# The last attention group with its probability-by-value products in pairs, each pair behind the scores of two steps

## What is computed

```python
xn = layernorm(x)
s = attention(xn)            # 32 heads of 16, ALiBi bias, causal softmax, output projection
g = silu(ffn(xn))            # three octonion-structured ternary linear layers
return x + s * g
```

```python
scores = q @ k.T * scale + alibi        # causal mask
attn = softmax(scores)
out[:, h] = attn @ v
s = out @ w_out.T + b_out
```

## Time and profile before

| | |
|---|---|
| median of 3 runs | 831.38 us (829.61 to 833.06) |
| the profiled execution | 832.83 us, of which the span of its instructions is 831.0 us |
| PE busy | 795.5 us (96%) |
| DVE busy | 607.0 us (73%) |
| ACT busy | 473.9 us (57%) |
| POOL busy | 172.2 us (21%) |
| granted PE clock, mean | 0.996 |

### The profile page before, as it was taken

The page is one execution under the profiler, slowest core; times in us unless marked ns, Lnnn a source line. Parts: engine busy times, 40 slices in busy tenths (PEclk is TensorE's granted clock), DMA queues, the critical chain, the costliest instruction groups (busy, mean ns, idle before and its releaser), DMA issues.

```text
span 831.0 us, 16157 instructions
## 1 busy us (share of the span) xinstructions
PE 795.5 (96%) x5927; PEld 351.1 (42%) x5927; DVE 607.0 (73%) x1743; ACT 473.9 (57%) x633; POOL 172.2 (21%) x214
## 2 busy tenths in 40 slices
PE   5989999999999999999899999999999999999988
PEld 3545444444444444444334343344443334443333
DVE  6736887643232463563799999999999999996546
ACT  6425384332232222232488898888888888887540
POOL 3223222233434424434200000000000003530000
PEclk9999999999999999999899999999999999999999
DMA  7474422268202101101121122222225233652736
GB/s 265 134 212 166 140 102 77 104 146 292 89 1 88 64 1 39 64 0 46 57 80 54 58 65 79 80 79 68 61 66 167 75 112 101 194 151 100 224 130 220
DMA packets 71104, 88.40 MB, mean 106 GB/s; under 512 B 26898, under 2 KB 37150, under 8 KB 70512
## 3 DMA queue, kind: packets, MB, share of 16 engines
q1 hardware_dynamic: 70992, 87.36, 32.9%
q0 software_dynamic: 32, 0.01, 0.0%
HBM read 51.15 MB, written 35.93 MB: 105 GB/s over the span
## 4 chain that ended last, share of the span: by engine, by line
PE 70%; DVE 17%; DMA 5%; issue 4%; ACT 2%; POOL 1%; SPq 0%; DVEq 0%; ACTq 0%
PE psum L1560 12%; PE psum L1583 9%; PE psum L1517 9%; PE psum L1584 9%; DVE mx L1235 9%; PE psum L1594 5%; PE psum L1595 5%; PE psum L1535 4%; DVE mshown L1231 3%; PE psum L1409 2%; PE psum L1411 2%; PE psum L1410 2%; PE psum L1544 1%; PE psum L1619 1%; DMA o_scr<-osum 1%
## 5 line engine op out<-in xcount | busy, mean ns | idle before, releaser
L949 ACT ACTIVATE probs<-psum,exp_scale 128x1024 f32<-128x1024 f32 (+1 forms) x320 | 310.6, 1029 | 69.7 <-PE psum L1544 49.9
L1231 DVE CUSTOM_DVE_ANT_0 mshown<-psum,ahead 128x384 bf16<-128x384 f32 (+3 forms) x512 | 220.3, 487 | 2.7 <-PE psum L1517 0.4
L1517 PE MATMUL psum<-QKs 51*128 51x512 f16 (+3 forms) x768 | 185.6, 332 | 15.0 <-DVE mx L1235 6.5
L1560 PE MATMUL psum<-probs,Vs 128*32 128x512 f32 (+3 forms) x1536 | 162.1, 510 | 0.2 <-ACT probs L949 0.2
L1235 DVE TENSOR_REDUCE mx<-psum 128x1 f32<-128x512 f32 x256 | 157.5, 681 | 2.7 <-PE psum L1517 1.7
L1535 PE MATMUL psum<-QKs 53*128 53x512 f16 (+3 forms) x768 | 138.2, 329 | 1.6 <-ACT probs L949 1.4
L1583 PE MATMUL psum<-X,room 128*128 128x512 f16 (+1 forms) x352 | 133.6, 379 | 0.0
L1584 PE MATMUL psum<-X,room 128*128 128x512 f16 (+1 forms) x352 | 133.4, 379 | 0.0
L1517 PEld LDWEIGHTS psum<-QKs 51*128 51x128 f16 x768 | 52.0, 93 | 151.4 <-DVE mx L1231 78.1
L981 ACT ACTIVATE room<-psum,gate_half 128x512 f32<-128x512 f32 (+1 forms) x44 | 30.2, 687 | 101.6 <-PE psum L1584 101.5
L1258 DVE SCALAR_TENSOR_TENSOR room<-room,psum 128x512 f32<-128x512 f32 (+1 forms) x44 | 30.2, 687 | 63.2 <-ACT room L981 63.2
(11 more groups left out here) (166 smaller groups left out, 964.6 us busy)
## 6 DMA issues: line engine op xcount, KB each, us to landing
o_scr<-osum SPq DMA_DIRECT2D x32, 256.0 KB, 3.1
QKs<-q_scr SPq DMA_DIRECT2D x96, 64.0 KB
QKs<-k_scr SPq DMA_DIRECT2D x96, 64.0 KB
q_scr<-qk_stage SPq DMA_DIRECT2D x16, 256.0 KB, 2.7
k_scr<-qk_stage SPq DMA_DIRECT2D x16, 256.0 KB, 2.2
v_scr<-v_stage SPq DMA_DIRECT2D x16, 256.0 KB, 2.1
Vs<-v_scr SPq DMA_DIRECT2D x16, 256.0 KB
probs<-in_L_attn_x SPq DMA_DIRECT2D x4, 1024.0 KB, 11.1
```

Of the source, the lines that this page charges most:

```text
L949: nc.scalar.activation(probs[n % PSLOTS][:, 2 * pair:2 * pair + 2, 0:COLS[n]], s_bank[pair][:, :, 0:COLS[n]], ACT.Exp, scale=exp_scale[:, ...
L1231: last = nc.vector.tensor_tensor_reduce(out=mshown[tiles_read(at) % 2][:, cols], in0=m_bank[bank][:, cols], in1=ahead[:, CH - keys:], scal ...
L1517: last = nc.tensor.matmul(tile[:, hh, :], Qs[s][rows, pair + hh, qb * P:(qb + 1) * P], Ks[s][rows, pair + hh, k0:k0 + keys], start=(hh == ...
L1560: last = nc.tensor.matmul(pv_bank[32 * h:32 * h + 32, CH - cols:CH], Vs[s][:, kb, h::QH], probs[n % PSLOTS][:, h, at:at + cols], start=(kb ...
```

## The change

In the last group the order no longer comes from `GROUP` but from a string of its own, `CLOSING`. In it an S stands for both pairs of a step, a P for the product run of one step. The work is the same, and so is the number of pieces of projection ahead of the scores; only the order differs. Products 8 and 9 of group 14 stand together, then 1 and 2, 3 and 4, 5 and 6, and 7, 8, 9 of group 15.

```diff
+CLOSING = "PSPPSSPSSPPSSPPSSPPS"
+
+
+def closing_order():
+
+    t = QUADS - 1
+    products = [(t - 1, n) for n in range(NST - LAG, NST)] + [(t, n) for n in range(NST - LAG)]
+    out, n = [], 0
+    for kind in CLOSING:
+        if kind == "P":
+            out.append(("products", *products.pop(0)))
+        else:
+            out += [("scores", t, n, pair) for pair in range(2)]
+            n += 1
+    return out
+
+
 def work_order():
 
...
             pieces.sort(key=lambda w: w != ("scores", 0, 0, 0))
+        if t == QUADS - 1:
+            pieces = closing_order()
         for w in pieces:
             if t == QUADS - 1 and w[0] == "scores":
                 for piece in range(behind, min(behind + 1 + (behind == 0), PIECES)):
```

## The result

| | kernel before | changed kernel |
|---|---|---|
| median | 830.92 us (20 runs) | 834.62 us (20 runs) |
| ratio of the times, 95% interval | | 1.0037 (1.0023 to 1.0052) |
| profiled execution | 832.83 us, span 831.0 us | 836.05 us, span 834.2 us |

The account below looks back on a forecast made before the run. PE, 96% busy, was taken to bound the kernel, its end hanging on the later of transfers and PE. PE's 1.51 us delay fitted into 1.72 spare: 831.38 plus 0 plus 0.2 gave 831.6 us, range 829.6 to 834.2.

Parts of the forecast that it names:

- likeliest case: End of the kernel: all delays absorbed, time 830 to 832.6 us; chance 0.72.
- Part 1: Two products in a row on PE: the second saves 0.18 us; a pair of 512 columns takes 1.88.
- Part 2: Group's head: moving product 8 of group 14 costs nothing; first exponential 0.43 us earlier, only ACT waits for PE there.
- Part 3: Products 1 and 2 of group 15: PE 0.18 us earlier, copy of chunk 0 and its store 1.55 us later.
- Part 4: Store of chunk 0 of group 15: queued behind token loads, so its later issue adds 0; bounds 0 and +1.55 us.
- Part 5: Steps 5 to 9 of group 15, ACT setting the pace: two waits of ACT make product 9 come 1.51 us later.
- PE's spare time: Projection row 8: PE's 1.72 us wait for transfers absorbs the 1.51 us delay; 0.2 us added for shorter waits.
- The clock rival: PE in 788 to 792: thin work halves the clock, 1.8 to 2.8 us net, time 833.2 to 834.2; chance 0.09.
- the store rival: Store of chunk 0: lands later, moving the closing transfers by up to 1.55 us, time 832.9; chance 0.12.

Follow-up runs that it names:

- e3: Changed kernel's order with throwaway matmuls added in PE's waits of steps 6 and 8 (2.4 us of work); ratio 1.0021 to the kernel before.
- e1: Kernel before with only the head changed: product 8 of group 14 moved from behind product 7 to before product 9; ratio 1.0003.
- e4: Kernel before with the last two token loads (2 MB) issued behind the reciprocals of chunk 0 of group 15; ratio 0.9990.
- e2: Kernel before with only steps 5 to 9 changed: products 3 and 4, and 5 and 6, paired behind four scores calls; ratio 1.0043.
- e5: Kernel before with products 3 to 6 of group 15 each one place later, none paired; ratio 1.0014.
- e7: Changed kernel's order with throwaway matmuls only in the first pair's waits (step 6), none in step 8; ratio 1.0052 to the kernel before.
- e8: Changed kernel's order with the last three of twelve projection pieces held back for PE's waits in steps 6 and 8; ratio 1.0003 to the kernel before.
- e6: Kernel before with the last two token loads (2 MB) issued behind the reciprocals of chunk 1 of group 15; ratio 1.0015.

## Why the prediction was wrong in its likeliest case and right in a rival

**Part 1, right at full clock.** Products 1 and 2 ran in one stretch of 1.46 us, as the changed kernel's timeline shows (784.65 to 786.11), and a pair of 512 takes 1.88 at full clock (e3):

```profile
784.65 1.53 PE L1579 MATMUL psum<-probs,Vs 128*32 128x256 f32 x24
786.11 0.39 PE L1638 MATMUL psum<-OW,room 128*128 128x512 f16 x1
```

**Part 2, not refuted by the times, wrong in its reason.** I wrote that nobody waits for the first scores but ACT. PE itself does, for the load of the row maxima, which I had not looked up. It was covered in five of six profiles and cost 1.03 us in the sixth. e1 shows no cost in the median.

**Part 3, right.** From the end of product 9 of group 14 to the first scores of step 5 it is 17.81 us (787.51 - 769.70) against 17.98 before. The store was issued 1.55 us later, counted from the same place (786.87 - 769.70 = 17.17 against 785.03 - 769.41 = 15.62); 1.55 was forecast.

**Part 4, right in its cause, open to about 1 us in its size.** e4 shows that the loads held the store. Whether the landing stayed where it was can't be read from one pair of profiles. Counted from the last scores of group 14, the load behind the store came at 34.26 us in the changed kernel, against 34.86 before. But in e1, e2 and e5, which issue the store at 23.4 as before, it came at 32.7 to 32.9, and in e3 and e7, which issue it at 24.96, at 33.6 and 34.0. In the changed kernel it did not matter, since PE came last.

**Part 5, right in form, short of the clock: the step that failed.** The waits of ACT cost 1.60 (e3), forecast 1.51. What failed is that this part costs PE's work behind a wait at the durations of rows at full clock: it has 1.88 us for each pair, and they took 3.29 and 3.57 at a clock of 0.50. The sum that I made was 1.51; the measured one is:
- head wait 1.09 (in this execution only);
- waits of ACT 1.60;
- clock under products 3 and 4: 42.36 - 39.66 = 2.70, less the 1.09 = 1.61;
- clock under products 5 and 6: 1.62.

These sum to 5.92. They close by construction: the first and third terms together are the distance between the changed kernel and e7. The first agrees with the timelines, where group 15's first scores come 5.26 us after the last ones of group 14 in the changed kernel and 4.16 in e1 and e7. PE's spare 1.72 takes up its part, which leaves 4.2 us, where the two spans differ by 4.0 from group 14 on.

**The sum's other step, PE's spare time, was too long.** I let 1.72 us take up the 1.51 and added 0.2 for executions with a shorter wait. The wait was 0.91 in e1, and e3, with the clock at full, is 0.3 to 3.2 us slower than the kernel before. So more than 0.2 shows even without the clock; how much is not settled.

**The rivals.** The clock rival named the place, the cause and the price, 1.8 to 2.8 us net for one long fall. In the profile there were two short ones, of some 3.4 us each, at 1.6 each. I gave it 0.09 and leaned on a row that did not compare: in the wait of 1.72 us the clock stayed, but PE was busy on both sides of it (2.00 of 2 us in 804 to 806, 1.89 in 808 to 810). The row that did compare was the one of 400 to 404, with 2.28 of 4 us busy and the clock at half behind it; my own schedule gave 2.4 of 4 us for 788 to 792, nearly that, and 2.39 were measured. It should have been a likely case. The Trainium skill, TensorE: Matmul & The Clock Gate, What's actually happening, says that the clock is throttled by default and released by activity; the runs agree: e3 adds 2.4 us of useless work and gets 1.6 us per pair back.
In the profile the store rival did not decide the end, and the pairs did save their 0.18 us at full clock.

**How well this gives the time.** With the clock's price from the traces and without the head's wait, the sum is 1.60 + 3.23 - 1.72 = 3.1 us, or 834.0 to 834.5 from the two medians of before. That is near the measured 834.62, but some of it is luck. With e1's 0.91 for the spare time it is 3.9. And the average execution lost less clock than the profiled one: the stretches of 790 to 802 add up to 3.4 us of full clock lost, 0.0041 of the span, where the mean clock of the changed kernel's 20 executions is 0.0022 below that of the kernel before in e1's measurement. That is worth 1.8 us by an estimate (0.0022 of 831), and the sum is 1.7 to 2.5. The measured 1.9 to 4.3 us do not decide between these.

## What to carry to other kernels

When an order groups work for its own sake, look at what stands ahead of the group: a stretch in which PE only issues short matmuls between waits for another engine is paid twice, once as wait and once at half clock in the dense work behind it. Price such a stretch by a place in the same trace that looks like it, short work between waits over several us, not by a single gap between busy stretches. If the order is wanted, keep independent work (here projection pieces) for the waits instead of spending it all earlier: e8 has the same pairs and no loss that its interval (0.15% to each side) can show. And where a forecast lets spare time on one path take up a loss on another, read that spare time from more than one execution.

## What the runs showed of the hardware

The granted clock fell to 0.50 behind stretches with 0.51 of 2 us busy (changed kernel) and 0.91 of 2 us (e5), and came back to 1.00 under dense products some 3 us later. In these runs it made a pair of float32 products 3.3 to 3.6 us instead of 1.88. It did not fall in the kernel before, with 1.39 of 2 us busy at 788 to 790, nor in e3, where the waits were filled. The share in one such stretch does not tell by itself: e1, e4 and e6 had 1.04 of 2 us in 788 to 790 and kept 1.00, and the kernel before had 0.39 in 806 to 808 and kept it, while e7 lost it behind 1.01 in 792 to 794:

```profile
788.00:790.00 2.00, 1.04 (x12) 0.31 (x10) 1.93 (x5) 2.00 (x3) 0.00 (x0) 1.00 1.01 378
790.00:792.00 2.00, 2.00 (x24) 0.54 (x18) 0.29 (x1) 2.00 (x2) 0.00 (x0) 1.00 0.57 219
```

These two rows are e1's.
